# One-hots of images 1 to 7 transposed by a DMA instead of on TensorE, with the counts taken from the transposed buffer

## The reference, cut to what matters

```
# x (8, 512, 32, 48), centroids (40, 512), W (512, 512), b (512), all float32
sim = einsum('bchw,nc->bnhw', x / |x|, centroids / |centroids|)
idx = argmax(sim, axis=1)
onehot = one_hot(idx, 40)                         # per image: 1536 tokens x 40
sum_x = einsum('bhwn,bchw->bnc', onehot, x)
count = sum(onehot, axis=(1, 2))
centroids_local = sum_x / maximum(count, 1.0)
gathered = centroids_local[b, idx]
delta = gathered - x
alpha = exp(-mean(delta * delta, channels))
y = x + alpha * delta
out = relu(einsum('oc,bchw->bohw', W, y) + b)
```

## Time and profile before

| | |
|---|---|
| three executions | 420.66, 421.40, 421.58 us; median 421.4 us |
| the profiled execution | 421.0 us |
| its span in the trace | 419.2 us |
| granted TensorE clock | 1.00, which is 2.4 GHz |
| TensorE matmuls busy | 410.0 us of the span |
| weight loads busy | 292.1 us |
| VectorE / ScalarE / GpSimd busy | 335.4 / 256.0 / 257.6 us |
| DMA | 73.94 MB, 63.2% of 16 engines' span |

### The profile page before, as it was taken

One profiled execution on the slowest core, in us unless ns is written; L12 is line 12 of the kernel. 1 busy time (PEld: TensorE's weight loads), 2 busy tenths in 40 slices (PEclk: granted clock), 3 DMA queues, 4 the chain that ended last, 5 costly groups with the idle time before them and its releaser, 6 DMA issues.

```text
span 419.2 us, 5853 instructions
## 1 busy us (share of the span) xinstructions
PE 410.0 (98%) x2127; PEld 292.1 (70%) x2150; DVE 335.4 (80%) x411; ACT 256.0 (61%) x351; POOL 257.6 (61%) x113
## 2 busy tenths in 40 slices
PE   7999999999999999999999999999999999999996
PEld 6744466775767767775868757777777758777885
DVE  2469979689789889899798898898798997788730
ACT  5665374665764765665855666746756658566641
POOL 2000654993599766993879936996769938334420
PEclk9999999999999999999999999999999999999999
DMA  8999295987389384966669573893857220222223
GB/s 275 309 277 159 55 255 155 297 243 179 123 212 291 102 211 147 275 172 179 223 154 253 195 198 104 237 265 121 220 136 228 100 102 1 102 100 100 96 77 128
DMA packets 70927, 73.94 MB, mean 176 GB/s; under 512 B 2724, under 2 KB 45732, under 8 KB 70900
## 3 DMA queue, kind: packets, MB, share of 16 engines
q1 hardware_dynamic: 70900, 73.58, 63.2%
HBM read 48.40 MB, written 25.17 MB: 175 GB/s over the span
## 4 chain that ended last, share of the span: by engine, by line
PE 90%; DVE 3%; ACT 3%; issue 1%; DMA 1%; SPq 0%; DVEq 0%; ACTq 0%
PE main L886 20%; PE main L887 19%; PE main L888 19%; PE sump L828 9%; PE fa L779 9%; PE gat L861 5%; DMA x<-x 1%; PE fa L788 1%; PE al L868 1%; PE fa L803 1%; DVE xt L350 1%; PE main L929 1%; PE al L874 1%; PE gat L874 1%; PE main L901 1%
## 5 line engine op out<-in xcount | busy, mean ns | idle before, releaser
L886 PE MATMUL main<-yh,wh 128*128 128x512 f32 x376 | 152.8, 406 | 0.7 <-ACT o L602 0.7
L887 PE MATMUL main<-yl,wh 128*128 128x512 f32 x376 | 146.7, 390 | 0.0
L888 PE MATMUL main<-yh,wl 128*128 128x512 f32 x376 | 146.7, 390 | 0.0
L310 POOL TENSOR_TENSOR z<-z,x 128x1024 f32<-128x1024 f32 x42 | 99.8, 2396 | 68.3 <-DVE z L437 68.3
L317 POOL TENSOR_TENSOR yl<-z,yh 128x1024 fp32r<-128x1024 f32 x44 | 105.6, 2420 | 54.9 <-ACT yh L594 54.9
L602 ACT ACTIVATE o<-main,bcol 128x512 f32<-128x512 f32 x96 | 65.3, 682 | 61.8 <-PE main L888 61.7
L886 PEld LDWEIGHTS main<-yh,wh 128*128 128x128 f32 x376 | 70.6, 188 | 21.9 <-issue 5.0
L888 PEld LDWEIGHTS main<-yh,wl 128*128 128x128 f32 x376 | 70.6, 188 | 15.2
L887 PEld LDWEIGHTS main<-yl,wh 128*128 128x128 f32 x376 | 70.7, 188 | 13.8
L324 POOL TENSOR_TENSOR xr<-xt 128x2048 f32<-128x2048 f32 x11 | 51.5, 4681 | 20.8 <-DVE xt L350 20.8
L413 DVE TENSOR_TENSOR z<-gat,x 128x1024 f32<-128x1024 f32 x46 | 56.1, 1219 | 9.3 <-PE gat L861 9.0
(11 more groups left out here) (118 smaller groups left out, 378.7 us busy)
## 6 DMA issues: line engine op xcount, KB each, us to landing
x<-x SPq DMA_DIRECT2D x24, 1024.0 KB, 5.4
out<-o SPq DMA_DIRECT2D x23, 1024.0 KB, 7.2
xs<-x SPq DMA_DIRECT2D x84, 256.0 KB, 5.6
o<-w SPq DMA_DIRECT2D x1, 1024.0 KB, 12.3
out<-o SPq DMA_DIRECT2D x4, 256.0 KB, 2.1
sq<-centroids SPq DMA_DIRECT2D x2, 80.0 KB
bcol<-bias SPq DMA_DIRECT2D x1, 2.0 KB, 11.9
```

Source lines behind the costliest of these rows:

```text
L310: pool.tensor_tensor(z, z, X[g // PARTS % 2][:, pair(h), span(g)], ALU.add).then_inc(y_pool, 1)
L886: t_.matmul(main[:, o % 2, :], WH[:, k, rows], YH[g % 2][:, k, :], start=(k == 0), stop=False)
L887: t_.matmul(main[:, o % 2, :], WH[:, k, rows], YL[g % 2][:, k, :], start=False, stop=False)
L888: last = t_.matmul(main[:, o % 2, :], WL[:, k, rows], YH[g % 2][:, k, :], start=False, stop=(k == KC - 1))
```

## The change

From image 1 on, TensorE's 12 transposes and ScalarE's evacuation are gone. In their place ScalarE issues one DMA behind `copy_onehot(b)`, which transposes all of `oh3` (128 partitions by 12 tiles by 128 columns, bf16, 384 KB) into `ohT[b % 2]`; its completion adds 16 to the new semaphore `ohT_in`, on which `gather` waits. The counts are made by `count_onehot(b)` on ScalarE: a copy of `ohT` into `simS`, whose content is not used, with the sum over the tokens in `accum_out`. It stands ahead of `copy_sums(b)` and waits for the DMA. `add_halves` waits for `ohT_done` no more. Since the DMA writes the tiles one after another, `ohT` now has its tokens in tile order: `slot` numbers the tiles by u and t, the similarities take their tokens in pieces of 32 from image 1 on (pieces of 64 before) and in two pieces of 128 in image 0, and `gather` reads `ohT` in 16 pieces of 32 columns. Image 0 keeps the transposes on TensorE.

```diff
+        def wait_onehot(eng, b):
+            if b == 0:
+                eng.wait_ge(ohT_done, 1)
+            else:
+                eng.wait_ge(ohT_in, 16 * b)
...
             def copy_onehot(b):
                 act.wait_ge(oh_done, b + 1)
-                wait(act, ohP_done, b)
+                if b > 0:
+                    if b == 1:
+                        act.wait_ge(ohP_done, 1)
+                    else:
+                        act.wait_ge(ohT_in, 16 * (b - 1))
...
+            def transpose_onehot(b):
+                act.wait_ge(oh3_done, b + 1)
+                wait(act, gat_done, 2 * PARTS * (b - 1))
+                act.dma_start_transpose(ohT[b % 2][:, :].rearrange("n (s i) -> n s i", i=P),
+                                        oh3[:, :, :].rearrange("p s n -> p (s n)")).then_inc(ohT_in, 16)
+
+            def count_onehot(b):
+                wait_onehot(act, b)
+                act.wait_ge(simT_done, b + 1)
                 wait(act, g_ready, b)
-                wait(act, gat_done, 2 * PARTS * (b - 1))
-                a_.activation(ohT[b % 2][:, :], ohP[0:NK, 0:HW], ACT.Copy, accum_out=count[:, :]
-                              ).then_inc(ohT_done, 1)
+                a_.activation(simS[:, :, :, :].rearrange("p u t s -> p (u t s)").bitcast(BF16)[0:NK, 0:HW],
+                              ohT[b % 2][:, :], ACT.Copy, accum_out=count[:, :]).then_inc(ohT_done, 1)
...
             copy_onehot(1)
+            transpose_onehot(1)
             exp(1)
             high_half(0, 0)
             high_half(0, 1)
+            count_onehot(1)
             high_half(1, 0)
             relu(0, 0)
             relu(0, 1)
             square(2, 0)
             copy_sums(1)
-            evacuate_onehot(1)
...
                 if beside and p == 2:
+                    count_onehot(b + 1)
                     copy_sums(b + 1)
-                    evacuate_onehot(b + 1)
...
                 if beside and p == 1:
                     copy_onehot(b + 1)
+                    transpose_onehot(b + 1)
...
                         if plain(b):
-                            toks = toks[:, h * HALF * P:(h + 1) * HALF * P]
+                            toks = toks.rearrange("p (t h i) -> p t h i", t=HALF, h=2)[:, :, h, :]
                         else:
-                            toks = toks.rearrange("p (q s) -> p q s", q=Q)[:, :, h * HALF * BLK:(h + 1) * HALF * BLK]
+                            toks = toks.rearrange("p (q t h i) -> p q t h i", q=Q, t=HALF, h=2)[:, :, :, h, :]
...
             def slot(u, t):
-                return (u * HALF + t % HALF) * 2 + t // HALF
+                return u * TILES + t
...
             def add_halves(b):
-                if b > 0:
-                    pe.wait_ge(ohT_done, b + 1)
...
-                pe.wait_ge(ohT_done, b + 1)
+                wait_onehot(pe, b)
...
+                toks = ohT[b % 2][:, span(g)]
+                if not plain(b):
+                    toks = toks.rearrange("n (t q i) -> n q t i", t=TILES, q=Q)
...
-                    transpose_onehot(b + 1)
                     convolve(g - LAG, 0)
                     add_halves(b + 1)
```

More of the change, by code:

```diff
@@ L167, in build @@
         arg_step, oh_done, oh3_done = sem("arg_step"), sem("oh_done"), sem("oh3_done")
-        ohP_done, ohT_done = sem("ohp_done"), sem("oht_done")
+        ohP_done, ohT_in, ohT_done = sem("ohp_done"), sem("oht_in"), sem("oht_done")
         tr_done, c_done, cop_done = sem("tr_done"), sem("c_done"), sem("cop_done")
@@ L616, in copy_onehot, with evacuate_onehot @@
                 act.wait_ge(oh_done, b + 1)
-                wait(act, ohP_done, b)
+                if b > 0:
[3 more added lines that the diff above has]
+                        act.wait_ge(ohT_in, 16 * (b - 1))
                 a_.activation(oh3[:, :, 0:USED].rearrange("p s (r n) -> p s r n", r=COPIES), oh[:, :, 0:N].unsqueeze(2).to_broadcast(
                     [P, PARTS * TILES, COPIES, N]), ACT.Copy).then_inc(oh3_done, 1)
-            def evacuate_onehot(b):
-                act.wait_ge(ohP_done, b + 1)
+            def evacuate_onehot():
+                act.wait_ge(ohP_done, 1)
+                a_.activation(ohT[0][:, :], ohP[0:NK, 0:HW], ACT.Copy, accum_out=count[:, :]
+                              ).then_inc(ohT_done, 1)
+            def transpose_onehot(b):
[6 more added lines that the diff above has]
+                act.wait_ge(simT_done, b + 1)
                 wait(act, g_ready, b)
-                wait(act, gat_done, 2 * PARTS * (b - 1))
-                a_.activation(ohT[b % 2][:, :], ohP[0:NK, 0:HW], ACT.Copy, accum_out=count[:, :]
-                              ).then_inc(ohT_done, 1)
+                a_.activation(simS[:, :, :, :].rearrange("p u t s -> p (u t s)").bitcast(BF16)[0:NK, 0:HW],
+                              ohT[b % 2][:, :], ACT.Copy, accum_out=count[:, :]).then_inc(ohT_done, 1)
             def copy_sums(b):
@@ L670, in _ @@
             copy_sums(0)
-            evacuate_onehot(0)
+            evacuate_onehot()
             high_weights(2)
@@ L791, in slot, with transpose_onehot @@
             def slot(u, t):
-                return (u * HALF + t % HALF) * 2 + t // HALF
[L794 to L803, removed]
+                return u * TILES + t
+            def transpose_onehot():
+                pe.wait_ge(oh3_done, 1)
+                for s in range(PARTS * TILES):
+                    last = t_.transpose(ohP[0:NK, s * P:(s + 1) * P], oh3[:, s, :], identb[:, :])
                 last.then_inc(ohP_done, 1)
@@ L858, in gather @@
                     pe.wait_ge(s_done, folded(g - 1))
+                toks = ohT[b % 2][:, span(g)]
+                if not plain(b):
+                    toks = toks.rearrange("n (t q i) -> n q t i", t=TILES, q=Q)
                 for j in range(2):
                     k = 2 * h + j
-                    last = t_.matmul(banks(g, h)[:, j, :], G[:, k * P:(k + 1) * P], ohT[b % 2][:, span(g)],
-                                     start=True, stop=True)
+                    last = t_.matmul(banks(g, h)[:, j, :], G[:, k * P:(k + 1) * P], toks, start=True, stop=True)
                 last.then_inc(gat_done, 1)
@@ L947, in _ @@
             sum_clusters(0, 2)
-            transpose_onehot(0)
+            transpose_onehot()
             transpose_weights(2)
@@ L978, in _ @@
             gather(2, 1)
-            transpose_onehot(1)
             convolve(0, 2, range(0, 2))
```

## The result

Four executions of the changed kernel took 434.50, 440.04, 443.35 and 444.70 us, median 441.7; before took 421.42 (four executions). The ratio is **1.0385, interval 1.0348 to 1.0421: slower**, by about 16 us; the median of all four is 20 us above before's. The executions differ among each other by far more than those of before do, and their mean granted TensorE clocks differ too: 0.992, 0.979, 0.976 and 0.977 in this order, where before had 1.00. The ratio leaves out the two longest executions; they are told of because their clock is low too. The profiled execution is the first, 434.5 us with a span of 432.7, so the trace shows the mildest case: 13.5 us more span than before.

What follows compares the result with a forecast made beforehand. TensorE was taken to bound the kernel; 421.0 us profiled, minus 5.1 for transposes, plus 0.4 for the issue at image 1, gave 416.3, and 416.7 us as the runs' median; range 415.5 to 432.

Steps and rivals of the forecast that it cites:

- What bounds the kernel: Whole loop: TensorE's list sets the pace, busy 48.43 of 48.63 us per image; VectorE has 5.5 us to spare.
- the transposes' worth: TensorE between gather and second convolution pass: removing 12 transposes saves 0.73 us in images 1 to 7, 5.1 us.
- The operands in small pieces: Similarities and gather on TensorE: reading operands in smaller pieces was taken to cost nothing.
- The issue: DMA issue on ScalarE: 1.44 us if by pieces, covered in the loop, +0.4 us once at image 1.
- The limit of 150.87: Latest start of ScalarE's count without TensorE waiting at add_halves, 4.95 us after the copy of the one-hots ends.
- six images pay: Images 2 to 7: each microsecond of landing beyond the limit was to cost 6 us.
- The DMA's landing: Transposing DMA beside SP's xs loads: lands after 4.7 us, at 150.6, without a wait, 0.25 us in hand.
- Rival 1: Late landing makes ScalarE wait at the count and TensorE at add_halves; 438.6 us at 8.6 us; chance 0.28.
- Rival 3: The DMA's twelve tiles go one after another, 25 us by rows, about 540 us in all; chance 0.06.

Runs made afterwards that it cites:

- e1: Kernel before with tokens in tile order alone (similarities in pieces of 32, gather in 16 pieces), transposes kept on TensorE: 420.94 us, ratio 1.0000.
- e6: Kernel before plus the same DMA in images 1 to 7, into a buffer nobody reads: 421.52 us, ratio 1.0012.
- e7: e3 with two ReLUs one place forward on ScalarE and image 1's DMA issued later: 416.20 us, ratio 0.9884 against before.
- e3: The changed kernel with the xs loads issued beside the DMA held by SP until it has landed: 419.77 us, ratio 0.9966 against before.
- e2: The changed kernel with the count moved on ScalarE to behind the unit's first ReLU: 434.32 us, ratio 1.0311 against before.
- e10: e7 with the hold on the loads taken out again: 435.18 us, ratio 1.0338 against before.

## Why the prediction was wrong

- **What bounds the kernel, and the transposes' worth: right.** 0.73 us per image, 5.1 in all, of which image 1 gave back 0.44 at `add_halves`, a wait that the forecast left out: 0.68 us from the gather to the second pass where 0.67 was expected, and an image's stretch of 47.88 us once nothing waits.
- **The operands in small pieces: right** (e1). **The issue: right in size and in place**: 1.49 us against 1.44, +0.4 at image 1 (0.41 us idle before L949), nothing in the loop (e6), though its reason, cost by pieces, was not.
- **The limit of 150.87, 4.95 us after the copy: right.** At the place of the forecast the DMA took 8.1 us from its issue, 3.1 over the limit, and TensorE waited 3.12. That six images pay was one too many: image 7 has no loads beside it any more, its DMA lands in 3.7 us, and TensorE doesn't wait.
- **The step that failed is "The DMA's landing".** I took 4.7 us, the landing of a 256 KB load in that stretch, as the nearest row; measured were 7.8 (8.3, 8.1, 8.1, 6.2 and 7.8 at images 2 to 6). The DMA's engine time would have allowed it: its packets take 3.9% of 16 x 432.7 us, 10976 of them, 25 ns each, not 45. But it landed with its last packets, and the row was no measure of it: on idle queues this DMA alone takes 3.7 us, where a 256 KB store took 2.1, and both the 2.1 and the 3.7 about double in this crowd (to 4.7 for a load, to 7.8 for the DMA). The loads pay too: with the DMA beside them the four of this stretch land after 6.6 us in place of 4.7. With 0.25 us in hand against an unknown that I myself bounded at 2.1 and 8.6 us, and at a cost of six times the lateness, the middle of the range was no forecast of "faster": above the limit lay more of the range than below.
- **Rival 1 is what happened**, at a landing of 7.8 us where it had 8.6 as its far end and 438.6 us as its price. The measured median, 441.7, lies above that because of what no case had: the clock, which falls to 1.2 GHz after some of the waits and takes 1.6 us each time, 3.5 us of the profiled execution and 9 to 11 of the others (estimates, above).
- **Rival 3 is out**: twelve tiles land in 3.7 us, not in 25. The Trainium skill ("VectorE: DVE Perf Modes", "The three transpose paths") gives 1309 ns for one 128x128 bf16 tile by DMA; twelve of them one after another would be 15.7 us, an estimate from that page, and the trace shows a quarter of it, since a further tile adds only 0.13 us. The advice in its "Rules for kernel authors", to transpose 128x128 on TensorE where a PSUM destination will do, held for the change as it stood (slower by 3.85%) and did not for e7 (faster by 1.16%).
- **ScalarE's list was taken as fixed.** I checked that the added work found room, and not that TensorE, 0.73 us earlier per image, would find its banks free: in e3 the ReLUs took back 0.5 of the 0.73.

## What to carry to other kernels

Moving work from a full engine to a DMA is worth what it removes only if the DMA lands before its first reader stands at the head of an in-order queue: work out that limit, and count the transfers that are issued within a microsecond of it, since their crowd doubled the landing here and a single wait in the loads' queue (e3) can clear it. Then look for what the engine that became faster meets next; here two ReLUs, one place too late, held most of the gain. And give a wait of 2 to 3 us on TensorE its clock as well: after some of them here the clock fell, which costs 1.6 us on top and makes the time scatter.

## What the runs showed of the hardware that was not expected

- A transpose by DMA of 384 KB of bf16 within SBUF lands 3.7 us after its issue on idle queues, and after 7.8 us (median; up to 9.2 in e2) beside 1 MB of loads in 512-byte pieces. It holds the issuing engine's queue for 1.2 us with 2 tiles and 1.5 with 12; SP's loads take 0.5 to 0.8.
- Its 256-byte packets take 25 ns each in the mean of the changed kernel (10976 packets, 3.9% of the span's 16 engines), so by engine time it is cheap; what is long is the time until the last of them is through: two microseconds for all 1568 on idle queues (e3), six beside the loads, two of these for the last 58.
- The length of a wait alone did not decide whether the clock fell to 1.2 GHz: in the changed kernel it fell after 2.95 and 2.87 us and not after 3.15, in e10 after 3.25 and not after 3.42, and in e2 after 1.81 and not after 1.78.
